# A decoder layer on one core: each head pair's weights scaled by their own sums of squares instead of by a scan of all weights

## The chip, the cores and the metric

The kernel runs on 1 core of a Trainium2 chip. The metric is device time in microseconds (us): the median of three runs of the kernel before is 2708.12 us (2706.8 to 2715.74).

## The reference

For 4 batches of 1024 tokens by 1024 features, x gets three updates, each after a layer norm without parameters:

```python
x = x + attn(norm(x))    # 16 heads of 64, causal; qkv = x @ w_qkv; softmax; out @ w_out
x = x + xattn(norm(x))   # softmax((ctx Wq + bq)(ctx Wk + bk)^T), 1024 x 1024, applied along the features
x = x + ffn(norm(x))     # 8 experts: gate by squared projections, best expert's rank-8 update, blended by the gate
```

Everything is float32. The kernel computes each large product with float16 pairs: an operand is a rounded high part plus the rounded rest, and a product is three matmuls (high by high, high by low, low by high). Float16 has a small range, so a weight tile is first multiplied by a power of two found from the weights themselves.

## The kernel before

The program is a list of steps per engine. Five strings per phase (`PE_START`, `DVE_START` and so on for the start; `..._BODY` for each head pair; `..._TAIL` for a batch's last pair with all that follows it) give the order on TensorE, VectorE (DVE), ScalarE (ACT), GpSimd (POOL) and the DMA queue of SyncE (SP). `walk` goes through them; a `+` after a name means the next pair, `++` the one after it; `ONCE` hangs further steps behind a step of one pair. Nothing reorders them: an engine that waits at a step holds back all its later ones. Attention goes by 8 head pairs per batch (n = 0 to 31; weights are prepared only for n below 8 and read back from DRAM copies later).

The start of batch 0 brings eight x tiles (128 tokens by 1024) into transposed pairs. For tile i: `AI` loads it, `AB` takes the statistics (DVE, bn), `AS` makes the scale and the shift (three tiny POOL instructions ve, rs, sh), `AX` normalizes (ACT), `AH` rounds (POOL, to probs), `AL` takes the rest (DVE, to probs), `AT` is a DMA transpose into `xt`. `x_in` has two slots, tile i + 2 is loaded after `AL` of tile i.

The weights of pair n are three tiles t = 0, 1, 2 (q, k, v; 128 x 1024): `WI` loads one to `w_raw` (two slots), `WH` rounds it with the scale `up_w` (POOL), `WL` takes the rest (DVE), `WS` stores the pair to DRAM. The scale is one for all q tiles, one for all k and one for all v, so the start first reads all 24 tiles of w_qkv: `SI` loads one into the large buffers r2 and r3 that attention needs later, `SR` takes its largest absolute value (DVE, tile_max, L985), and `SC1` to `SC3` reduce eight such columns (a PE transpose, a maximum, a power of two: `scale`, L887 to L911). w_out's eight tiles are scanned in pairs 0 and 1 (four SI loads behind `T1`, four SR behind `R6`), and prepared in pairs 3 to 6 (VI, VH, VL, VS).

`P t h` is a projection: 24 matmuls of 512 columns for weight tile t and half h of the tokens, in four parts; `CH` (ACT) and `CL` (DVE) move its result to float16 pairs. Then for the row blocks q = 0 to 7 of a pair: `S q` scores (PE), `X q` row maxima (DVE; the first of a pair is L850 of shape 128x128), `E q` exp with its sum (ACT, two instructions), `R q` reciprocals, `H q` rounding (POOL, pn), `L q` rest (DVE, pn), `T q` DMA transpose of pn (two slots), and `M0`, `M1` the products with v, with `OH` and `OL` behind them. `V` is the DMA transpose of v. `constants` (`CS`) builds the expert constants: 16 float32 matmuls and the scale of the expert weights.

Of the kernel before, what the change touches and what calls it, by code (L numbers as in the profile page):

```python
# [122 lines left out]
for pair in range(3, 7):
    u, v = 2 * pair - 6, 2 * pair - 5
    ONCE["SP", pair, "T1"] = f"VI{u} VI{v}"
    ONCE["POOL", pair, "H31"] = f"VH{u} VH{v}"
    ONCE["DVE", pair, "R4"] = f"VL{u} VL{v}"
    ONCE["SP", pair, "T5"] = f"VS{u} VS{v}"
# [11 lines left out]
def decoder_layer(nc, x, w_qkv, w_out, ctx_t, w_ctx, b_ctx, w_ffn, v_ffn, w_up, center, slope, out):  # L140
    es = ExitStack()
    with es:
# [19 lines left out]
        neg_half = sb(es, "neg_half", [P, 1])  # L162
        bias_c = sb(es, "bias_c", [P, 2])
        tile_max = sb(es, "tile_max", [P, 40])
        part_max = sb(es, "part_max", [P, 8])
        whole_max = sb(es, "whole_max", [P, 8])
        least_max = sb(es, "least_max", [P, 8])
        power = sb(es, "power", [P, 8])
        inverse = sb(es, "inverse", [P, 8])
        up_w = sb(es, "up_w", [P, 8])  # L170
        back = sb(es, "back", [P, 4])
        sc, c_out, c_ffn, c_ffn2 = (back[:, i:i + 1] for i in range(4))
# [163 lines left out]
        def proj_bank(n, h):  # L336
            return ps_s[:, 0, half(h)] if n % PAIRS == 0 else ps_p[:, h, :]

        def scale_bank(j):
            return ps_p[:, 0, 0:P] if j < 4 else ps_o[:, 1, 0:P]  # L340
# [42 lines left out]
        with nc.Block() as block:  # L383

            @block.sync
            def _(sp):
# [53 lines left out]
                def rest(kind, a, b):  # L440
                    if kind == "SI":
                        j, i = a
                        if j < 3:
# [9 lines left out]
                        return
# [761 lines left out]
```

## Time and profile before

| what | value |
|---|---|
| median of 3 runs | 2708.12 us |
| profiled execution | 2711.69 us, span 2709.8 us |
| PE busy | 2395.8 us (88%) |
| DVE busy | 1890.0 us (70%) |
| ACT busy | 780.1 us (29%) |
| POOL busy | 713.2 us (26%) |
| DMA | 403.97 MB, mean 149 GB/s |

Busy times are shares of the whole span. PE at 88% on average says little about the first 5% of the span: the profile's slices show PE at 0, 5, 8, 8 tenths there and 9 in most later ones. The stages must be read apart, and the times in them refer to the span's start.

### The profile page before, as it was taken

How to read it: one execution, taken by the hardware profiler on the slowest of the kernel's cores; microseconds unless marked ns; L12 is line 12 of the kernel's file. 1: busy time of each engine (PE TensorE's matmuls, PEld its weight loads, DVE VectorE, ACT ScalarE, POOL GpSimd, SP SyncE). 2: the span in 40 equal slices, each digit the busy share in tenths (PEclk: the TensorE clock that was granted, in tenths of full speed). 3: DMA queues.
4: the chain of work that ended last, by engine and by line, in shares of the span. 5: the costliest groups of instructions: out<-in, count | busy, mean ns of one | idle time of the engine just before them, and what ended most of it. 6: DMA issues, size and time to landing. Idle time of an engine off the chain costs nothing.

```text
span 2709.8 us, 37859 instructions
## 1 busy us (share of the span) xinstructions
PE 2395.8 (88%) x14389; PEld 1180.2 (44%) x14389; DVE 1890.0 (70%) x3421; ACT 780.1 (29%) x1557; POOL 713.2 (26%) x981
## 2 busy tenths in 40 slices
PE   0588888799898999979988999979989999988997
PEld 0233434354454444445444444445444444435544
DVE  4577877756876777765785777675696777765566
ACT  1033333321213333332212333342121333342110
POOL 3132433213402222212421222222430222222220
PEclk6799999899999999989998999989999999998997
DMA  6677778866746676786753777685773677777543
GB/s 174 227 179 170 170 199 200 210 148 146 145 105 126 138 145 142 146 201 139 154 118 100 143 143 145 143 197 128 160 146 107 119 145 146 142 149 185 109 78 93
DMA packets 986009, 403.97 MB, mean 149 GB/s; under 512 B 937116, under 2 KB 946332, under 8 KB 985828
## 3 DMA queue, kind: packets, MB, share of 16 engines
q1 hardware_dynamic: 985828, 401.56, 67.4%
q8 instruction: 114, 1.87, 0.3%
q14 instruction: 67, 0.55, 0.1%
HBM read 133.05 MB, written 33.55 MB: 61 GB/s over the span
## 4 chain that ended last, share of the span: by engine, by line
PE 60%; DVE 19%; DMA 9%; issue 5%; ACT 3%; POOL 2%; SPq 1%; ACTq 0%; POOLq 0%; DVEq 0%
PE ps_p L538 8%; PE ps_p L540 8%; PE ps_p L539 8%; DMA r<-pn 7%; PE ps_s L538 7%; PE ps_s L539 7%; PE ps_s L540 7%; PE ps_s L583 6%; PE ps_o L608 5%; DVE pn L817 4%; DVE peak L854 2%; ACT probs L743 2%; DVE bn L822 2%; DMA qk<-in_x 2%; PE ps_s L588 1%
## 5 line engine op out<-in xcount | busy, mean ns | idle before, releaser
L1081 POOL TENSOR_SCALAR pn<-probs,rden 128x640 f16<-128x640 f32 (+7 forms) x512 | 388.9, 772 | 1294.5 <-DVE rden L866 774.2
L743 ACT ACTIVATE probs<-ps_s,low,back 128x640 f32<-128x640 f32 (+7 forms) x512 | 421.4, 826 | 887.3 <-DVE low L857 775.8
L817 DVE SCALAR_TENSOR_TENSOR pn<-probs,rden,pn 128x640 f16<-128x640 f32 (+7 forms) x512 | 474.6, 959 | 170.1 <-POOL pn L1081 170.1
L538 PE MATMUL ps_p<-r,w 128*128 128x512 f16 x1344 | 514.5, 383 | 2.6 <-DVE qk L817 2.6
L539 PE MATMUL ps_p<-r,w 128*128 128x512 f16 x1344 | 513.9, 382 | 0.0
L540 PE MATMUL ps_p<-r,w 128*128 128x512 f16 x1344 | 513.5, 382 | 0.0
L583 PE MATMUL ps_s<-qk 64*128 64x512 f16 (+3 forms) x2304 | 245.5, 339 | 118.6 <-ACT probs L743 108.6
L854 DVE TENSOR_REDUCE peak<-ps_s 128x2 f32<-128x1280 f32 (+3 forms) x128 | 241.4, 1886 | 40.5 <-PE ps_s L588 37.6
L608 PE MATMUL ps_o<-r,vn 128*64 128x512 f16 (+3 forms) x2304 | 213.2, 342 | 44.2 <-issue 43.7
L583 PEld LDWEIGHTS ps_s<-qk 64*128 64x128 f16 x2304 | 91.8, 97 | 266.3 <-ACT probs L743 156.7
L540 PEld LDWEIGHTS ps_p<-r,w 128*128 128x128 f16 x1344 | 132.3, 98 | 161.7 <-issue 5.3
L608 PEld LDWEIGHTS ps_o<-r,vn 128*64 128x64 f16 x2304 | 141.3, 114 | 132.8 <-issue 80.6
L538 PE MATMUL ps_s<-r,pn 128*128 128x512 f16 x512 | 195.0, 381 | 0.0
L540 PE MATMUL ps_s<-r,pn 128*128 128x512 f16 x512 | 194.7, 380 | 0.0
L539 PE MATMUL ps_s<-r,pn 128*128 128x512 f16 x512 | 194.7, 380 | 0.0
L538 PEld LDWEIGHTS ps_p<-r,w 128*128 128x128 f16 x1344 | 132.5, 99 | 142.2 <-DVE qk L817 4.5
L539 PEld LDWEIGHTS ps_p<-r,w 128*128 128x128 f16 x1344 | 132.4, 98 | 137.4 <-issue 4.0
L538 PE MATMUL ps_s<-r 128*128 128x512 f16 x384 | 146.0, 380 | 0.0
L539 PE MATMUL ps_s<-r 128*128 128x512 f16 x384 | 145.6, 379 | 0.0
L540 PE MATMUL ps_s<-r 128*128 128x512 f16 x384 | 145.6, 379 | 0.0
L863 DVE TENSOR_SCALAR den_s<-den 128x2 f32<-128x2 f32 x256 | 42.5, 166 | 134.1 <-ACT probs L743 134.1
L1085 POOL TENSOR_SCALAR ve<-mv 128x1 f32<-128x1 f32 x96 | 28.5, 296 | 399.0 <-DVE mv L825 397.5
(167 smaller groups left out, 3532.0 us busy)
## 6 DMA issues: line engine op xcount, KB each, us to landing
w<-w_pairs SPq DMA_DIRECT2D x72, 512.0 KB, 3.9
qk<-in_x SPq DMA_DIRECT2D x32, 512.0 KB, 4.3
r<-wo_pairs SPq DMA_DIRECT2D x16, 1024.0 KB, 6.6
w_raw<-in_x SPq DMA_DIRECT2D x32, 512.0 KB, 4.1
out<-r SPq DMA_DIRECT2D x32, 512.0 KB, 2.9
r<-in_w_qkv SPq DMA_DIRECT2D x24, 512.0 KB, 5.7
w_raw<-in_w_qkv SPq DMA_DIRECT2D x24, 512.0 KB, 5.8
w_pairs<-w SPq DMA_DIRECT2D x24, 512.0 KB, 5.5
```

The costliest lines, as they stand in the source:

```text
L538: pe.matmul(ps, lh, rh, start=start and k == ks[0], stop=False)
L539: pe.matmul(ps, lh, rl, start=False, stop=False)
L540: mm = pe.matmul(ps, ll, rh, start=False, stop=stop and k == ks[-1])
L583: pe.matmul(ps_s[:, j, to.start + c:to.start + d], qk_part(n, 0, qs, block_of(q))[rows(j), :], qk_part(n, 1, ks, slice(c, d))[rows(j), :], ...
L608: mm = pe.matmul(ps_o[rows(j), g, c:HALF], vn[:, n % 2, vs, kb, rows(j)], keys_of(g, j, s, kb), start=kb == 0 and vs == 0 and s == 0, stop ...
L743: act.activation(probs_part(q, j, w), ps_s[:, j, scores(q)], ACT.Exp, bias=low[:, n % 2, i:i + 1], scale=sc, accum_out=den[:, n % 2, i:i + ...
L817: dve.scalar_tensor_tensor(out=to, in0=bank, scalar=scale, in1=rounded, op0=ALU.mult, op1=ALU.subtract).then_inc(ok, 1)
L822: ins = dve.bn_stats(bn[:, T % 2, h, :], src[:, half(h)])
L854: dve.tensor_reduce(peak[:, n % 2, r], ps_s[:, :, scores(q)], AX_X, ALU.max).then_inc(peak_ok, 1)
L863: dve.tensor_scalar(den_s[:, n % 2, r], den[:, n % 2, r], 1.0 / UP_A, None, ALU.mult).then_inc(den_ok, 1)
L1081: pool.tensor_scalar(to, src, scale, 1.0, ALU.mult, ALU.mult).then_inc(ok, 1)
L1085: pool.tensor_scalar(ve, mv[:, 1:2], EPS, UP_X ** -2, ALU.add, ALU.mult).then_inc(ok_ve, 1)
```

## The change

The scan of w_qkv goes. ACT takes the sum of squares of each raw tile of a pair (`WN`, activation Square with `accum_out`, written beside into scratch called junk), three PE transposes (`WC` on PE) and a chain of small DVE instructions (`WC` on DVE, `own_scales`) make the pair's own three powers of two from it. Pair n + 2 is treated in the body of pair n, pairs 0 and 1 in the start. The softmax scale is one column per pair (`sc(n)`). The eight x tiles of batch 0 have eight slots (`x1`, in r2, free now), so their loads wait for nothing. Pair 0 projects P00, P10, P20 first (first half of the tokens) and then P01, P11, P21; its two banks alternate by `turn_of`. The expert constants move behind the last x tile. w_out is still scanned for one common scale, together with the v tiles of pairs 4 to 7, by ACT (`SI`, `SN`, twelve tiles in pairs 0 and 1). `WI`, `WS` and `VI` stand at other places between the transposes `T`. From batch 1 on nothing changes.

DVE, start, around x tile 3: before (bn, mv: statistics of an x tile; tile_max: the scan; probs: `AL`).

```order
L985 TENSOR_REDUCE tile_max<-r 128x1
L1002 TENSOR_TENSOR probs<-qk_1,probs 128x1024
L822 BN_STATS bn<-qk_1 128x6 x2
L825 BN_AGGR mv<-bn 128x2
L985 TENSOR_REDUCE tile_max<-r 128x1
L1002 TENSOR_TENSOR probs<-qk_1,probs 128x1024
```

Now, with the scale chain of pair 0 (c_peak, c_low and c_den_s are its temporaries, sizes holds the scales):

```order
L883 BN_STATS bn<-r 128x6 x2
L886 BN_AGGR mv<-bn 128x2
L1089 TENSOR_TENSOR probs<-r,probs 128x1024
L950 TENSOR_REDUCE c_peak<-ps_o 128x3
L953 TENSOR_SCALAR c_low<-c_peak 128x3
L955 TENSOR_SCALAR sizes<-c_low 128x3
L960 RECIPROCAL c_den_s<-sizes 128x3
L966 TENSOR_SCALAR sizes<-c_den_s 128x3
L967 TENSOR_SCALAR sizes<-sizes 128x1
L883 BN_STATS bn<-r 128x6 x2
L886 BN_AGGR mv<-bn 128x2
L1089 TENSOR_TENSOR probs<-r,probs 128x1024
```

The scan's row is gone from each tile's turn, and one chain of six small rows stands between tiles.

ACT, end of pair 0: before (probs: `E`; qk, vt: `CH`).

```order
L743 ACTIVATE probs,den<-ps_s,low,back 128x896 x2
L732 ACTIVATE qk_1<-ps_p 128x512
L743 ACTIVATE probs,den<-ps_s,low,back 128x1024 x2
L732 ACTIVATE vt<-ps_p 128x512
L743 ACTIVATE probs,den<-ps_s,low,back 128x128 x2
L732 ACTIVATE vt<-ps_p 128x512
```

Now, with the sums of squares of scanned tiles (L813, from xn and t):

```order
L796 ACTIVATE probs,den<-ps_s,low,sizes 128x896 x2
L813 ACTIVATE r,sizes<-xn 128x8x128
L776 ACTIVATE qk_1<-ps_p 128x512
L796 ACTIVATE probs,den<-ps_s,low,sizes 128x1024 x2
L813 ACTIVATE r,sizes<-t 128x8x128 x2
L776 ACTIVATE vt<-ps_p 128x512
L796 ACTIVATE probs,den<-ps_s,low,sizes 128x128 x2
L776 ACTIVATE vt<-ps_p 128x512
```

Two sums stand between the last exp of the pair and the copy of v's first half.

The DMA queue (SP), first half of pair 1: before (r<-pn: `T`; 128x4x128 is T0, 128x8x128 T1).

```order
L424 DMA_TRANSPOSE r<-pn 128x4x128
L424 DMA_TRANSPOSE r<-pn 128x8x128
L452 DMA xn<-in_w_out 128x1024 x2
L452 DMA t<-in_w_out 128x1024 x2
L401 DMA w_pairs<-w 128x2048
L395 DMA w_raw<-in_w_qkv 128x1024
L424 DMA_TRANSPOSE r<-pn 128x12x128
L424 DMA_TRANSPOSE r<-pn 128x16x128
```

Now:

```order
L454 DMA_TRANSPOSE r<-pn 128x4x128
L475 DMA xn<-in_w_out 128x1024
L475 DMA t<-in_w_out 128x1024
L475 DMA t<-in_w_qkv 128x1024
L431 DMA w_pairs<-w 128x2048
L454 DMA_TRANSPOSE r<-pn 128x8x128
L426 DMA w_raw<-in_w_qkv 128x1024
L454 DMA_TRANSPOSE r<-pn 128x12x128
L431 DMA w_pairs<-w 128x2048
L426 DMA xn<-in_w_qkv 128x1024
L454 DMA_TRANSPOSE r<-pn 128x16x128
```

Four transfers stand ahead of T1 instead of none, five ahead of T2 instead of six, and seven ahead of T3 instead of six. In pair 2 it is one, two and four instead of none, two and two.

The diff, cut:

```diff
 ACT_BODY = """
-    E00 E01 CH21 E10 E11 E20 E21 CH00+ E30 E31 OH1- E40 E41 CH01+ E50 E51 CH10+ OH0 E60 E61 CH11+ E70 E71
+    E00 E01 CH21 E10 E11 WN0++ E20 E21 CH00+ WN1++ E30 E31 OH1- E40 E41 CH01+ WN2++ E50 E51 CH10+ OH0 E60 E61
...
 PE_START = """
-    CS SC0 SC1 P000+ P001+ P002+ P003+ P010+ P011+ P012+ P013+ SC2 P100+ P101+ P102+ P103+ P110+ P111+ P112+ P113+
-    SC3 P200+ P201+ P202+ P203+ P210+ P211+ P212+ P213+ S0+ S1+
+    WC+ P000+ P001+ P002+ P003+ P100+ P101+ P102+ P103+ P200+ P201+ P202+ P203+ CS SC0 P010+ P011+ P012+ P013+
+    P110+ P111+ P112+ P113+ WC++ P210+ P211+ P212+ P213+ S0+ S1+
 DVE_START = """
+    AB0+ AB1+ AL0+ AB2+ AL1+ AB3+ AL2+ AB4+ AL3+ WC+ AB5+ AL4+ WL0+ AB6+ AL5+ WL1+ AB7+ AL6+ WL2+ CL00+ AL7+ CL10+
+    CS CL20+ SC0 CF CL01+ CL11+ WC++ CL21+ WL0++ WL1++
 ACT_START = """
+    AX0+ AX1+ AX2+ WN0+ AX3+ WN1+ AX4+ WN2+ AX5+ AX6+ AX7+ CH00+ CH10+ CH20+ CH01+ WN0++ WN1++ CH11+ WN2++ CH21+
 POOL_START = """
+    AS0+ AS1+ AH0+ AS2+ AH1+ AS3+ AH2+ AS4+ AH3+ WH0+ AS5+ AH4+ WH1+ AS6+ AH5+ WH2+ AS7+ AH6+ AH7+ CF WH0++ WH1++
 SP_START = """
+    AI0+ AI1+ WI0+ AI2+ WI1+ AI3+ WI2+ AI4+ AI5+ AT0+ AI6+ AT1+ AI7+ AT2+ CS AT3+ AT4+ AT5+ AT6+ AT7+ WI0++ WI1++
+    WI2++ WS0+ WS1+ WS2+ WS0++ V+
...
+for pair, first in ((0, 0), (1, 6)):
+    for at, row in (("T0", (0, 1, 2)), ("T4", (3,)), ("T5", (4,)), ("T6", (5,))):
+        ONCE["SP", pair, at] = " ".join(f"SI{first + e:02d}" for e in row)
+    for at, row in (("E31", (0,)), ("E41", (1,)), ("E51", (2,)), ("E61", (3,)), ("E71", (4, 5))):
+        ONCE["ACT", pair, at] = " ".join(f"SN{first + e:02d}" for e in row)
...
+        def turn_of(n, t, h):
+            return 6 * n + (3 * h + t if n == 0 else 2 * t + h)
+        def raw(n, t):
+            if n == 0 or n == 1 and t == 2:
+                return first_raw[:, 3 if n else t, :]
+            return w_raw[:, t, :] if t < 2 else xn3[:, 1, :]
+        def x_in(T):
+            return x1[:, T, :] if T < TB else c_probs[:, T % 2, :]
...
                     if kind == "WI":
-                        if k >= 2:
-                            sp.wait_ge(w_ok, k - 1)
+                        if n >= 3 or n == 2 and t < 2:
+                            sp.wait_ge(w_ok, 3 * n + t - 2)
...
+                    elif kind == "WC":
+                        pe.wait_ge(own_ok, 3 * n + 3)
+                        for t in range(3):
+                            mm = pe.transpose(ps_o[:, 1, block_of(t)], sum_of(n, t).broadcast_to([P, P]), ident[:, :])
+                        mm.then_inc(own_turn, 1)
...
+                    elif kind == "WN":
+                        act.wait_ge(w_in[t], 16 * (n + 1))
+                        act.activation(junk(n), raw(n, t).rearrange("p (t d) -> p t d", t=TB), ACT.Square, scale=NORM,
+                                       accum_out=sum_of(n, t)).then_inc(own_ok, 1)
...
+                if kind == "SN":
+                        act.wait_ge(scan_in[e % 3], 16 * (e // 3 + 1))
...
+                def own_scales(n):
+                    c = 3 * n
+                    dve.wait_ge(own_turn, n + 1)
+                    powers(slice(c, c + 3), (ps_o[:, 1, 0:3 * P], True), own_step, 4 * n)
+                    dve.tensor_scalar(up_w[:, c:c + 3], inverse[:, :], 2.0 ** 13, None, ALU.mult)
+                    dve.tensor_scalar(sc(n), power[:, c:c + 1], power[:, c + 1:c + 2], 2.0 ** -15, ALU.mult,
+                                      ALU.mult)
```

## Rows read from the trace of the kernel before

**Rows 1.** Windows: PE, PEld, DVE, ACT, POOL busy, clock, DMA share, GB/s.

```profile
0.00:136.60 136.60, 42.72 (x180) 19.83 (x180) 69.28 (x102) 14.79 (x15) 34.44 (x59) 0.71 0.65 199
136.60:512.50 375.90, 327.69 (x2072) 150.23 (x2072) 292.74 (x460) 125.62 (x278) 131.46 (x138) 0.97 0.78 182
189.00:248.10 59.10, 47.72 (x305) 22.61 (x306) 44.15 (x69) 18.10 (x40) 17.54 (x20) 0.97 0.75 178
248.10:299.40 51.30, 47.42 (x305) 21.42 (x305) 41.55 (x72) 18.31 (x40) 18.55 (x20) 0.97 0.76 157
817.20:1150.70 333.50, 317.69 (x2068) 146.61 (x2070) 237.42 (x417) 126.37 (x278) 82.28 (x112) 0.99 0.71 139
```

**Rows 2.** Chain of waits, one x tile: start, us, engine and tile.

```profile
26.25 3.96 DMA qk<-in_x
30.23 1.30 DVE bn L822 x2
...
31.76 1.08 DVE tile_max L985
32.84 1.14 DVE probs L1002
```

**Rows 3.** Timeline of x tiles: start, us, engine, line, work [idle before, releaser].

```profile
4.48 1.29 DVE L822 BATCH_NORM_STATS2 bn<-qk 128x6 f32<-128x512 f32 x2 [4.48 <-DMA qk<-in_x]
...
22.30 0.27 POOL L1089 TENSOR_SCALAR sh<-mv,rs 128x1 f32<-128x1 f32 x1
...
23.92 1.04 POOL L1081 TENSOR_SCALAR probs<-qk 128x1024 f16<-128x1024 f32 x1
...
32.77 1.34 POOL L1089 TENSOR_SCALAR sh<-mv,rs 128x1 f32<-128x1 f32 x1
...
34.14 1.24 ACT L759 ACTIVATE qk<-qk,sh,rs 128x1024 f32<-128x1024 f32 x1 [9.03 <-POOL sh L1089]
```

**Rows 4.** Timeline from the scan's first scale to the first row maxima.

```profile
76.59 0.47 PE L630 MATMUL ps_p<-ident,part_max 128*128 128x128 f32 x1 [58.65 <-DVE part_max L884]
...
78.33 1.12 POOL L1081 TENSOR_SCALAR w<-w_raw,up_w 128x1024 f16<-128x1024 f32 x1 [3.12 <-DVE up_w L901]
...
79.55 1.28 DVE L817 SCALAR_TENSOR_TENSOR w<-w_raw,up_w,w 128x1024 f16<-128x1024 f32 x1 [1.39 <-POOL w L1081]
...
80.89 0.61 PE L538 MATMUL ps_s<-r,w 128*128 128x512 f16 x1 [3.83 <-DVE w L817]
...
87.86 0.60 ACT L732 ACTIVATE qk<-ps_s 128x512 f16<-128x512 f32 x1 [13.78 <-PE ps_s L540]
...
93.04 0.60 ACT L732 ACTIVATE qk<-ps_s 128x512 f16<-128x512 f32 x1 [4.58 <-PE ps_s L540]
...
136.60 0.28 DVE L850 TENSOR_REDUCE peak<-ps_s 128x1 f32<-128x128 f32 x1
```

**Rows 5.** Timeline of the expert constants on PE.

```profile
12.08 3.95 PE L617 MATMUL ps_p<-ffn_prod,ones 128*128 128x136 f32 x16 [12.08 <-DVE ffn_prod L919]
```

**Rows 6.** Chain of waits in pair 0: the scan of w_out.

```profile
175.66 4.49 DVE tile_max L985 x4
```

**Rows 7.** Timelines of DVE and SP at the end of pair 0.

```profile
182.79 2.28 DVE L854 TENSOR_REDUCE peak<-ps_s 128x2 f32<-128x2048 f32 x1
...
182.89 4.25 SPq L424 DMA_TRANSPOSE r<-pn  x1
```

**Rows 8.** Timelines of POOL in pair 1, and of SP and ACT in pair 2.

```profile
222.04 1.57 POOL L1081 TENSOR_SCALAR pn<-probs,rden 128x640 f16<-128x640 f32 x2 [10.68 <-DMA r<-pn]
...
271.15 19.62 SPq L424 DMA_TRANSPOSE r<-pn  x4
...
275.71 0.99 ACT L743 ACTIVATE probs<-ps_s,low,back 128x768 f32<-128x768 f32 x1 [3.03 <-DVE low L857]
```

**Rows 9.** DMA issues: KB each, median us to landing.

```profile
w_raw<-in_w_qkv SPq DMA_DIRECT2D x24, 512.0 KB, 5.8
```

**Rows 10.** Timeline of ACT at the start.

```profile
0.71 1.28 ACT L759 ACT_TABLE_LOAD   x1 [0.71 <-PEq L1208]
```

More of the change, by code:

```diff
@@ L32 @@
 UP_X, UP_A = 2.0 ** 10, 2.0 ** 14
-Q_OUT = 2.0 ** -19
+NORM = 2.0 ** -24
+Q_OUT = 2.0 ** -17
 O_OUT = 2.0 ** -14
@@ L121 @@
+for pair in range(3, 7):
+    u, v = 2 * pair - 6, 2 * pair - 5
+    ONCE["SP", pair, "T0"] = f"VI{u}"
+    ONCE["DVE", pair, "R1"] = f"VF{u}"
+    ONCE["POOL", pair, "H31"] = f"VH{u}"
+    ONCE["DVE", pair, "R4"] = f"VL{u}"
+    ONCE["SP", pair, "T4"] = f"VI{v}"
+    ONCE["POOL", pair, "H61"] = f"VH{v}"
+    ONCE["SP", pair, "T5"] = f"VS{u}"
+    ONCE["DVE", pair, "R7"] = f"VL{v}"
+    ONCE["SP", pair, "T7"] = f"VS{v}"
 for pair in range(PAIRS - 2, BATCH * PAIRS, PAIRS):
     ONCE["SP", pair, "T6"] = "JI0 JI1 KI"
[L123 to L128, printed above, removed]
@@ L161, in decoder_layer @@
         rank = sb(es, "rank", [P, EXPERTS])
[L162 to L172, printed above, removed]
+        sizes = sb(es, "sizes", [P, 104])
+        squares, power, up_w, back = sizes[:, 0:36], sizes[:, 36:63], sizes[:, 63:90], sizes[:, 90:101]
+        neg_half, bias_c = sizes[:, 101:102], sizes[:, 102:104]
+        c_out, c_ffn, c_ffn2 = (back[:, PAIRS + i:PAIRS + i + 1] for i in range(3))
         bn1, bn2, bn3 = (sb(es, f"bn{s}", [P, 2, 2, 6]) for s in (1, 2, 3))
@@ L274, in decoder_layer @@
         m_ok, oh_ok, o_ok = sems("m_ok oh_ok o_ok")
+        a_first = [sem(f"a_first{s}") for s in range(TB)]
         a_in = [sem(f"a_in{s}") for s in range(2)]
@@ L334, in scores, with proj_bank, junk, sum_of @@
             return slice(base, base + (q + 1) * P)
[L336 to L340, printed above, removed]
+        def turn_of(n, t, h):
+            return 6 * n + (3 * h + t if n == 0 else 2 * t + h)
+        def proj_bank(n, t, h):
+            return ps_s[:, 0, half(turn_of(n, t, h) % 2)] if n % PAIRS == 0 else ps_p[:, h, :]
+        def raw(n, t):
[4 more added lines that the diff above has]
+            return x1[:, T, :] if T < TB else c_probs[:, T % 2, :]
+        def junk(n):
+            return pt[:, 8 * SEQ:9 * SEQ].rearrange("p (t d) -> p t d", t=TB) if n < 2 else o16[:, :, 0, PAIRS - 1, :]
+        def sum_of(n, t):
+            c = 8 * t + n if n < 4 or t < 2 else 32 + n - 4
+            return squares[:, c:c + 1]
+        def scan_sum(e):
+            c = 24 + e if e < 8 else 12 + e
+            return squares[:, c:c + 1]
+        def scale(n, t):
+            return up_w[:, 3 * n + t:3 * n + t + 1]
+        def sc(n):
+            return back[:, n % PAIRS:n % PAIRS + 1]
         def ctx_bank(t):
@@ L750, in attend @@
                         if n == 0:
-                            act.wait_ge(scan_ok, 24)
+                            act.wait_ge(a_lo, TB)
                         act.activation(heads_out(g, 0, p), heads_bank(g), ACT.Copy, scale=O_OUT).then_inc(oh_ok, 1)
                 def rest(kind, a, b):
+                    if kind == "SN":
+                        e = 10 * a[0] + a[1]
+                        act.wait_ge(scan_in[e % 3], 16 * (e // 3 + 1))
+                        if e > 0:
+                            act.wait_ge(scan_ok, e)
+                        act.activation(o16[:, :, 1, PAIRS - 1, :], wo_scan[e % 3].rearrange("p (t d) -> p t d", t=TB), ACT.Square,
+                                       scale=NORM, accum_out=scan_sum(e)).then_inc(scan_ok, 1)
+                        return
                     i, = a if a else (0,)
```

293 lines of the change are left out of this document (155 added, 138 removed), and 3 rows, old and new, of the table ONCE.

## The prediction

> **What bounds the kernel now.** I first cut the span into stages by windows [rows 1]. PE is busy for 42.7 of the first 136.6 us, for 327.7 of the 375.9 us of pairs 0 to 6, and for 317.7 of the 333.5 us of the same seven pairs in batch 1. So the start is 94 us of PE idle, batch 0's pairs carry 42 us more than those of batch 1, and from there on PE is nearly full and the change touches nothing. The limit at 136.6 is the first row maxima of pair 0 (X0) [rows 4]; all that the start must deliver is in front of it.
>
> Then the chain of waits for one x tile [rows 2]: load 3.96, statistics 1.30 (with their sum to 31.76), scan 1.08, rest 1.14, and the next load starts. That is a ring of 7.7 us because a slot is loaded only after its rest: the scan and the load are both in it. The projections [rows 4]: the first scale's transpose is at 76.59, POOL's rounding at 78.33, the matmuls start at 80.89, the first result is moved at 87.86, the next at 93.04. A group of 24 matmuls thus takes 5.2 us when PE comes from work and 7.0 after an idle time. The groups of k and v wait for the scans of 16 more tiles; last of all X0 at 136.60.
>
> **The start after the change.** With eight slots the load leaves the ring; the scan leaves it too. What is left per tile is in the written orders: on DVE `AB(i+1) AL(i)`, on POOL `AS(i+1) AH(i)`. So AH(i) stands behind AS(i+1), that behind AB(i+1), and that behind AL(i-1): a ring of statistics 1.5, three POOL instructions 1.3 (1.0 from the end of the statistics at 31.76 to sh at 32.77, and 0.27 for a free sh), rounding 1.04, rest 1.22 [rows 2, 3], with gaps 5.2 us. The normalization (1.24) runs a tile ahead and is hidden.
>
> First tile: lands at 4.48 [rows 3], and 1.5 + 1.3 + 1.25 + 1.1 + 1.2 gives its rest at 11. Three rings: tile 3 done at 26.5.
> Scales of pair 0: the third sum of squares, a 1024-column activation like the normalization (1.25, and about 0.1 for its accumulator), ends at about 27. The old chain needs 1.74 from transpose to POOL [rows 4]; three transposes and three rows wide I take 3: POOL starts at 30.
> Tiles 4 to 6 with one WH and one WL each: DVE does AB, AL, WL (1.5 + 1.2 + 1.28), POOL AS, AH, WH (1.2 + 1.04 + 1.12), in a ring of 6.3 that now has WL in it: WL2 ends at 30 + 3 x 6.3 = 49.
> PE: P00 and P10 are done by then. P20 also needs the rest of P00 (0.7 behind WL2): 49.6 to 54.8. The constants stand behind it: their DVE work is done by 53, so PE has them from 54.8 to 58.8 (3.95 us [rows 5]), and 0.8 for a copy and a transpose. P01 and P11: 10.4 us to 70.0. Tile 7's transpose, issued at about 51, has landed long before. Then PE stands at `WC++` for the third sum of squares of pair 1, which ACT takes only behind the copy of P11: 0.6 + 1.35 and semaphores, plus three transposes of 0.3, 3.3 us in all. P21 5.2 to 7.0, its move 1.4, and two WL (2.4) ahead of X0: 73.3 + 6.1 + 1.4 + 2.4 = 83.
>
> So X0 goes from 136.6 to 83: **53.6 us less**. Bounds: if WL and AL hide and PE goes straight on, 76; if each of the eight tiles goes on costing 7.7 us, the last rest is at 73 instead of 51 and X0 at 105. I take 83, since every term has a row.
>
> A port rule bears on this. In the trace POOL's sh takes 1.34 us instead of 0.27 when it meets DVE's rest [rows 3]. The Trainium skill (SBUF — State Buffer, Who interferes with whom) says that a DVE instruction with two SBUF inputs and a GpSimd instruction that reads SBUF exclude each other, the first to issue keeping the port, while tensor_reduce never contends; by that rule the removed scan never slowed POOL, and each WL and AL that remains can hold a WH or AH for up to its 1.2 us. The trace agrees with the first half: beside the scan (31.76 to 32.84 [rows 2]) ve and rs are done by 32.77 [rows 3]. My ring has DVE and POOL mostly one behind the other, so the sum holds by the row; by the rule at its worst, six such holds put X0 at 90.
>
> **The pairs of batch 0.** Removed: four DVE scans in pair 0 and four in pair 1, 4.49 us on the chain [rows 6]: -4.5 each, -9 together. Moved on SP: in pair 1 T2 stood behind six transfers, and POOL waited 10.68 us for it [rows 8]; with five ahead, but three of them issued before T1, T1 is late instead. I take -3 for pair 1, and -4 for pair 0, where T1 comes late anyway and only one load is left ahead of T2.
>
> Added, in the order of the body. (1) `WN2++` on ACT in front of E50: its tile is loaded behind T2. In pair 2 T2 is issued from 271.15 [rows 8], so the load goes at about 275 and lands at 279 to 281 (5.8 us is its median [rows 9]); with 1.35 for the sum, E50 starts at about 281 instead of 275.71 [rows 8]. Queued behind it on ACT are E50, E51 and the copies, and PE's S6 waits for E51. But PE has P and M0 there until about 280 and DVE is at L40 and L41, so of the 5 us I count 1.5. (2) The chain `WC++` on DVE between X6 and L50, 1.5 us, of six pairs (n = 0 to 5). X6 now stands ahead of L50, so E6 runs beside it: L50 and T5 are later by 3 or more, X7 by about 1.5. I count 1 to 2. Together +3 in pair 2 and, where VI was already in the way and is now split, +1 each in pairs 3 to 5. (3) At the end of pairs 0 and 1 ACT has SN04 and SN05 in front of `CH20+`. SI05 is issued behind T6; T6 took 4.25 us to issue, from 182.89, when X7 began at 182.79 [rows 7]. So the load goes at 4.4 us after X7's start, lands at 8 and its sum ends at 9.5; copy and rest, then X0 of the next pair at 10.5 instead of 6.2 (189.0 less 182.8 [rows 1, 7]). I count 3.5 of the 4.3, since POOL gets ahead meanwhile: +7 for the two.
> (4) ACT as an engine has room: 125.6 busy of 375.9 us [rows 1], and 30 more sums add 40.
>
> Sum per pair: 0: -4.5 - 4 + 3.5 + 2 = -3; 1: -4.5 - 3 + 3.5 + 1 = -3; 2: +3; 3 to 5: +3; 6: 0. **Zero in all.** Bounds: -17 if all seven pairs fall to the 51.3 us of pair 2, which had no scan loads; +20 if the sums of squares cost their full 5 us in pairs 1 to 5 (the ends of the unshown waits).
>
> Profiled execution 2711.7 less 53.6 is 2658; it lies 3.6 above the median, and the same difference from the median 2708.1 gives 2654.5. I say **2655**.
>
> **Rivals.**
> *The start stays slow.* Loads, stores and transposes share the queue; SP needs about 3.5 us per transpose, and if POOL waits for the probs slots each tile costs 7.7 again: X0 at 105, time 2677. For it: the DMA share was 0.65 over the start [rows 1]. Against: that share was mostly the scan's 12 MB, which is gone. 10%.
> *The pairs gain too.* If the scattered transfers shorten the wait for T2 (10.68 in pair 1, while pair 2 without scan loads takes 51.3 against 59.1 [rows 1]), batch 0's seven pairs lose 12 to 18 us: 2637 to 2643. For it: the difference of pairs 1 and 2. Against: the same megabytes, and four v tiles more. 15%.
> *Slower.* ACT in front of E50 behind a load: the place is `WN2++` in six pairs and SN in two. It decides from 54 / 6 = 9 us lost per pair; with the longest wait for a transfer in the trace, 10.7 us, in each, 64 us come back and the time is 2719. Against: PE and DVE cover part of each wait. 3%.
> *Table switches.* If Square and Exp did not share ACT's function table, each of some 28 groups of sums among the exps would bring two loads, of 1.28 us as the one at the start took [rows 10]: 72 us in front of exps that PE waits for, and a time of 2709 to 2727. The Trainium skill (ScalarE: Activation LUTs, Table sets: the hidden batching unit) tells to batch activations by table set for that reason, and with its about 2.7 us a switch it would be more. The changed program has one table load on ACT, as before, so 1%, at about 2720.
> *It doesn't do what it says:* the first tile's chain takes as long because constants and x share the queue: X0 no earlier than 125, 2697. 2%.
>
> **How the numbers follow.** The forecast holds 69%: 2645 to 2668. Two kernels within 0.3% (8 us) can't be told apart. Slower by more: the 3% and the 1%. Within: 1%, from a slow start and slow pairs together. Faster: 95%. The range for 8 in 10 takes in the pair bounds and half of the slow start: 2634 to 2676.
>
> **What would show it.** Right: X0 of pair 0 (the 128x128 row maxima on ps_s) at 83 +- 5; x tiles' rests spaced 5.2 us, later 6.3; PE idle for 2 to 3 us before the last projection of pair 0; ACT idle before sums of squares waiting for a DMA; pairs 0 to 6 in 370 to 380 us; everything after pair 7's start as long as before (2197 us from there to the end of the span). Wrong: X0 above 95, or the pairs' sum off by more than 15.

## The result, and the profile after: slower, with the start as forecast and the pairs far off

| what | before | after |
|---|---|---|
| median | 2709.14 us (2706.8 to 2715.74, 4 runs) | 2749.32 us (2739.13 to 2750.7, 4 runs) |
| ratio | | 1.0136, 95% interval 1.0106 to 1.0167 |
| profiled execution | 2711.69 us, span 2709.8 | 2750.7 us, span 2748.8 |

The forecast was 2655 with a range of 2634 to 2676: the change was expected to save 54 us and cost 40. The windows of the kernel after, cut at the first row maxima (X0) of pairs 0, 1, 2, 3 and 7 (columns as in [rows 1]), show where:

```profile
0.00:79.80 79.80, 39.02 (x183) 18.10 (x183) 43.08 (x70) 21.01 (x27) 26.59 (x59) 0.99 0.66 178
79.80:143.80 64.00, 48.60 (x259) 20.59 (x259) 36.01 (x67) 26.46 (x56) 17.78 (x19) 0.82 0.71 171
143.80:220.40 76.60, 52.41 (x307) 23.09 (x307) 39.26 (x70) 27.43 (x58) 17.09 (x19) 0.81 0.68 152
220.40:286.20 65.80, 48.93 (x302) 22.03 (x303) 40.71 (x78) 21.10 (x46) 14.32 (x17) 0.86 0.57 124
...
549.80:2748.80 2199.00, 2032.55 (x12132) 1010.24 (x12130) 1513.25 (x2863) 640.07 (x1264) 547.16 (x786) 0.96 0.65 140
```

```profile
79.80:549.80 470.00, 347.85 (x2098) 155.78 (x2099) 286.76 (x493) 156.39 (x338) 133.01 (x137) 0.86 0.67 150
```

The start went from 136.6 to 79.8 us, 56.8 less. Pairs 0 to 6 went from 375.9 [rows 1] to 470.0, 94.1 more. Everything from pair 7's first row maxima on takes 2199.0 instead of 2709.8 - 512.5 = 2197.3. Sum: -56.8 + 94.1 + 1.7 = +39.0, the difference of the two spans. Pair 2 alone takes 65.8 us instead of 51.3 [rows 1], with 302 matmuls in its window against 305.

**The start.** Its rows answer to [rows 2 to 4]. Timeline of the kernel after (start, us, engine, line, work, idle time before and its releaser): statistics of two x tiles, the first scale's maxima, the first rounding, the first projection, two rests and a rounding behind the second; then the constants and the end of the start.

```profile
10.72 1.28 DVE L883 BATCH_NORM_STATS2 bn<-r 128x6 f32<-128x512 f32 x2
...
15.69 1.28 DVE L883 BATCH_NORM_STATS2 bn<-r 128x6 f32<-128x512 f32 x2
...
26.76 0.56 DVE L950 TENSOR_REDUCE c_peak<-ps_o 128x3 f32<-128x384 f32 x1 [1.05 <-PE ps_o L606]
...
28.38 1.12 POOL L1168 TENSOR_SCALAR w<-r,sizes 128x1024 f16<-128x1024 f32 x1 [3.92 <-DVEq L969]
...
32.23 1.12 POOL L1168 TENSOR_SCALAR w<-r,sizes 128x1024 f16<-128x1024 f32 x1
32.28 2.14 DVE L1089 TENSOR_TENSOR probs<-r,probs 128x1024 f16<-128x1024 f32 x1 [2.31 <-POOL probs L1168]
...
35.67 0.61 PE L563 MATMUL ps_s<-r,w 128*128 128x512 f16 x1 [8.95 <-DVE w L878]
...
46.44 1.23 DVE L1089 TENSOR_TENSOR probs<-r,probs 128x1024 f16<-128x1024 f32 x1 [2.31 <-POOL probs L1168]
...
46.76 1.80 POOL L1168 TENSOR_SCALAR probs<-r 128x1024 f16<-128x1024 f32 x1 [0.36 <-ACT r L820]
...
55.49 2.02 PE L659 MATMUL ps_p<-ffn_prod,ones 128*128 128x136 f32 x16
...
70.36 0.54 PE L606 MATMUL ps_o<-ident,sizes 128*128 128x128 f32 x3 [1.72 <-ACT r L784]
...
77.42 2.47 DVE L878 SCALAR_TENSOR_TENSOR w<-w_raw,sizes,w 128x1024 f16<-128x1024 f32 x2
...
79.81 0.29 DVE L914 TENSOR_REDUCE peak<-ps_s 128x1 f32<-128x128 f32 x1
```

The ring of an x tile is 15.69 - 10.72 = 4.97 us (worked out: 5.2), POOL's first rounding starts at 28.38 (30), P20 runs from 50.3 (49.6), two WL stand in front of X0, and X0 is at 79.81 (83). With a WL in it the ring is longer than forecast: the rests of x tiles 4 and 5 start at 32.28 and 39.36, 7.1 us apart (6.3), which eats up the earlier start of the weights. The 3.2 us by which X0 is early come mainly from two terms. The constants took 2.02 us instead of the 3.95 of [rows 5], and PE stood at `WC++` for less: P21 starts 2.1 us after the end of P11 (3.3 were counted), 1.72 of them idle.

**The pairs.** The groups of waits between 79.8 and 549.8 (engine, tile, line, what it waited for: us in total, times, longest):

```profile
PE ps_s L623 <- ACT probs L796: 117.8, 29, 15.8
...
ACT r L784 <- DMA w_raw<-in_w_qkv: 96.8, 12, 11.2
...
ACT r L784 <- DMA xn<-in_w_qkv: 30.7, 6, 5.7
```

The same view of the kernel before, from 136.6 to 512.5:

```profile
PE ps_s L583 <- ACT probs L743: 34.8, 26, 3.3
```

L784 is the sum of squares. ACT stands 18 times in front of it, 127.5 us in all, and PE's wait for the exps grew from 34.8 to 117.8. The timelines of SP, ACT, PE and DVE in pair 2 show the three places, and what PE and DVE make of them:

```profile
223.58 4.88 SPq L454 DMA_TRANSPOSE r<-pn  x1
228.56 2.03 SPq L459 DMA_TRANSPOSE vn<-vt  x1
230.65 0.91 SPq L426 DMA_DIRECT2D w_raw<-in_w_qkv  x1
236.63 1.19 SPq L454 DMA_TRANSPOSE r<-pn  x1
...
240.15 1.23 SPq L454 DMA_TRANSPOSE r<-pn  x1
241.43 0.57 SPq L426 DMA_DIRECT2D w_raw<-in_w_qkv  x1
252.90 1.43 SPq L454 DMA_TRANSPOSE r<-pn  x1
...
255.28 0.42 SPq L426 DMA_DIRECT2D xn<-in_w_qkv  x1
```

```profile
234.83 1.06 ACT L784 ACTIVATE r<-w_raw 128x1024 f16<-128x1024 f32 x1 [8.25 <-DMA w_raw<-in_w_qkv]
235.79 0.19 ACT L784 ACTIVATION_READ_ACCUMULATOR r<-w_raw 128x1 f32 x1
235.89 0.65 ACT L796 ACTIVATE probs<-ps_s,low,sizes 128x384 f32<-128x384 f32 x1
...
245.20 1.06 ACT L784 ACTIVATE r<-w_raw 128x1024 f16<-128x1024 f32 x1 [7.43 <-DMA w_raw<-in_w_qkv]
...
261.21 1.06 ACT L784 ACTIVATE r<-xn 128x1024 f16<-128x1024 f32 x1 [5.13 <-DMA xn<-in_w_qkv]
```

```profile
232.13 4.41 PE L650 MATMUL ps_o<-r,vn 128*64 128x512 f16 x48
...
247.92 1.78 PE L623 MATMUL ps_s<-qk 64*128 64x512 f16 x12 [11.38 <-ACT probs L796]
```

```profile
239.64 0.48 DVE L878 SCALAR_TENSOR_TENSOR pn<-probs,rden,pn 128x256 f16<-128x256 f32 x1
```

Read them together. SP issues T7, V, then WI0 at 230.65; the tile lands at 234.8, and `WN0++`, which stands in front of E20, has held ACT for 8.25 us by then. WI1 is issued at 241.43, behind T1; `WN1++`, in front of E30, ends its wait at 245.20, and PE, which had nothing left after `M1-` (L650, to 236.54), has by then idled most of its 11.38 us for exps. WI2 stands behind T2 and holds E50 for 5.13 us. Behind each sum stand exps whose scores are ready, behind these PE's next scores, DVE's reciprocals and rests, and behind those the next transpose and so the next load. T1 is an example: it is issued at 240.15, right behind DVE's rest of row block 1 (L11, 239.64 + 0.48 = 240.12). That rest stands in DVE's list behind R2, which needs the exps that `WN0++` had held.

### The profile page after: what moved, and what is told of

It reads as the page before. It is cut to its first block, busy times and chain, and to the rows that moved or that the text cites. A ratio compares the mean times of both kernels' runs of the same rounds, so it can differ in the third digit from the quotient of the medians.

```text
span 2748.8 us, 38004 instructions
## 1 busy us (share of the span) xinstructions
PE 2419.4 (88%) x14411; PEld 1184.1 (43%) x14411; DVE 1843.1 (67%) x3423; ACT 817.5 (30%) x1629; POOL 706.8 (26%) x981
## 4 chain that ended last, share of the span: by engine, by line
PE 56%; DVE 19%; DMA 9%; issue 7%; ACT 4%; POOL 3%; SPq 2%; ACTq 0%; POOLq 0%; DVEq 0%
PE ps_p L563 8%; PE ps_p L564 8%; PE ps_p L565 8%; DMA r<-pn 7%; PE ps_s L563 7%; PE ps_s L564 6%; PE ps_s L565 6%; PE ps_s L623 6%; DVE pn L878 5%; PE ps_o L650 4%; ACT probs L796 3%; DVE peak L918 2%; DMA w_raw<-in_w_qkv 2%; DVE bn L883 2%; PE ps_s L628 1%
## 5 line engine op out<-in xcount | busy, mean ns | idle before, releaser
L796 ACT ACTIVATE probs<-ps_s,low,sizes 128x640 f32<-128x640 f32 (+7 forms) x512 | 420.9, 825 | 824.4 <-DVE low L921 714.6
L878 DVE SCALAR_TENSOR_TENSOR pn<-probs,rden,pn 128x640 f16<-128x640 f32 (+7 forms) x512 | 455.1, 926 | 140.2 <-POOL pn L1168 138.8
L563 PE MATMUL ps_p<-r,w 128*128 128x512 f16 x1344 | 520.6, 387 | 2.4 <-DVE qk L878 2.4
L564 PE MATMUL ps_p<-r,w 128*128 128x512 f16 x1344 | 520.3, 387 | 0.0
L565 PE MATMUL ps_p<-r,w 128*128 128x512 f16 x1344 | 519.0, 386 | 0.0
L650 PE MATMUL ps_o<-r,vn 128*64 128x512 f16 (+3 forms) x2304 | 212.5, 341 | 30.9 <-issue 30.8
L650 PEld LDWEIGHTS ps_o<-r,vn 128*64 128x64 f16 x2304 | 133.5, 114 | 125.8 <-issue 67.1
```

The lines of the kernel that those rows point to most:

```text
L563: pe.matmul(ps, lh, rh, start=start and k == ks[0], stop=False)
L564: pe.matmul(ps, lh, rl, start=False, stop=False)
L565: mm = pe.matmul(ps, ll, rh, start=False, stop=stop and k == ks[-1])
L650: mm = pe.matmul(ps_o[rows(j), g, c:HALF], vn[:, n % 2, vs, kb, rows(j)], keys_of(g, j, s, kb), start=kb == 0 and vs == 0 and s == 0, stop ...
L796: act.activation(probs_part(q, j, w), ps_s[:, j, scores(q)], ACT.Exp, bias=low[:, n % 2, i:i + 1], scale=sc(n), accum_out=den[:, n % 2, i: ...
L878: dve.scalar_tensor_tensor(out=to, in0=bank, scalar=scale, in1=rounded, op0=ALU.mult, op1=ALU.subtract).then_inc(ok, 1)
```

## Experiments

Each experiment edits the changed kernel unless it says otherwise. Those run once are judged by the length of pairs 0 to 6 in the profile, since a single total can't settle a few us. The start is 79.6 to 79.9 us in all of them. Everything from pair 7 on is the same work in all of them; it took 2186.7 to 2199.0 us, 0.6% apart. If the pairs scatter by the same share, that is 2 to 3 us (an estimate), so differences of that size between two windows say little.

**All loads of the sums early (e1).** On SP only (the start's list gets one more `WI0+++` at its end):

```diff
-    WD2+ WI0++ T0 WS1+ T1 WI1++ T2 WS2+ WI2++ T3 T4 WD0++ T5 T6 WS0++ WD1++ T7 V+
+    WD2+ WI1++ WI2++ T0 WS1+ T1 T2 WS2+ T3 T4 WD0++ T5 T6 WS0++ WI0+++ WD1++ T7 V+
```

> Only the SP order differs from the changed kernel: of pair n + 2 the loads WI1 and WI2 stand ahead of T0 and WI0 stands ahead of T7 of the body before, instead of WI0 ahead of T0, WI1 behind T1 and WI2 behind T2. The same sums, chains and transfers remain. Theory A (ACT stands at WN0, WN1 and WN2 for loads that SP issues only behind gated transposes; 96.8 + 30.7 us of such waits in pairs 0 to 6): nearly all waits go, pairs 0 to 6 fall from 470 us to 375 to 400, the time to 2655 to 2680. Rival B (the sums as work on ACT, 30 x 1.25 us, and the scale chain cost it): waits go, but the pairs stay above 450, time 2730 to 2750. Rival C (stores and loads ahead of T1 to T3 delay the transposes): only a part, 430 to 450, time about 2715.

2680.38 us (2671.18 to 2682.98, 4 runs) against 2710.61 of the kernel before: ratio 0.9894 (0.9877 to 0.9912). Window of pairs 0 to 6, and the waits in it:

```profile
79.80:480.40 400.60, 338.53 (x2098) 151.78 (x2099) 288.99 (x493) 156.05 (x338) 137.38 (x137) 0.94 0.76 176
```

```profile
ACT r L784 <- DMA w_raw<-in_w_qkv: 27.5, 6, 6.5
```

Same instructions, same bytes, another place in one queue: 470.0 becomes 400.6, so 69.4 of the 94.1 us come with the late loads (the medians are 68.9 apart). Theory A had 375 to 400 and at most 2680, and the run lies at that edge; B and C are far off. The wait for a tile in `xn` (WI2) is gone from the list. For tiles in `w_raw` ACT still waits 27.5 us, so not every wait went.

**No sums from pair 2 on (e2), and no scale chain either (e3).** The loads stay where the changed kernel has them. The main lines of the edits; the waits and columns that go with them are left out:

```diff
 e2, ACT, step WN:
-                        if n >= PAIRS:
+                        if n >= 2:
 e3 besides, DVE, step WC (PE's the same; the scales are those of pair n % 2):
-                        if n < PAIRS:
+                        if n < 2:
```

> The changed kernel without the sums of squares of pairs 2 to 7 (their scales come from the sums of pairs 0 and 1, the common one of v and w_out from half the tiles); loads, stores, chains and w_out's sums stay where they are. Theory A and rival B both expect pairs 2 to 5 to lose their excess (about 68 us each now, then 52 to 56), total near 2670; only against e1 does it tell the waits from the work: A expects e1 and this one within 15 us, B expects this one 40 us or more below e1. Rival C expects pairs 2 to 5 to stay at 62 or more.

> As the one without the sums of pairs 2 to 7, and without their scale chains on PE and DVE too (all take the scales of pairs 0 and 1). The difference to it is the price of six chains, 1.5 us of DVE each: theory A expects 0 to 9 us less (1 to 2 per pair), a rival that sees PE and DVE held at the chain expects 20 us or more.

Windows of pairs 0 to 6, e2 and then e3:

```profile
79.60:479.50 399.90, 341.20 (x2098) 153.39 (x2099) 290.63 (x492) 138.91 (x302) 136.62 (x137) 0.93 0.77 176
```

```profile
79.80:467.30 387.50, 333.73 (x2080) 149.83 (x2081) 279.15 (x457) 138.53 (x302) 137.47 (x137) 0.95 0.79 182
```

Taking the sums away (399.9) and loading for them early (400.6) come to the same, as theory A said; rival B wanted 40 us between them. So neither ACT's 17 us of work for the sums, nor the 27.5 us that ACT still waits in e1, nor a late load that only POOL's WH needs (e2) shows a cost. That two of these cancel is not excluded. The loads are as late in e2 as in the changed kernel, and the pairs are fast all the same: late transfers by themselves, rival C, are not the cause; the sums in front of the exps are. The six chains in pairs 0 to 5 cost 12.4 us, 2.1 each; 0 to 9 had been expected, and 20 or more by the rival. (Totals of the single runs: 2674.29 and 2661.04.)

**Only WI2 late (e6); only WI0 early (e9); only WI1 early (e10).**

```diff
 e6, from e1:
-    WD2+ WI1++ WI2++ T0 WS1+ T1 T2 WS2+ T3 ...
+    WD2+ WI1++ T0 WS1+ T1 T2 WS2+ WI2++ T3 ...
 e9:
-    WD2+ WI0++ T0 WS1+ ... T6 WS0++ WD1++ T7 V+
+    WD2+ T0 WS1+ ... T6 WS0++ WI0+++ WD1++ T7 V+
 e10:
-    WD2+ WI0++ T0 WS1+ T1 WI1++ T2 ...
+    WD2+ WI0++ WI1++ T0 WS1+ T1 T2 ...
```

> As e1, but the load WI2 of pair n + 2 stays behind T2 as in the changed kernel; WI0 and WI1 are early. It isolates the one ACT wait that the prediction priced (WN2 ahead of E50: 5 us late, 1.5 counted). By that price pairs 0 to 5 are 9 us above e1 (400.5), at 410; if the full wait falls on the path, 30 above, at 430; the rest of the 70 us between the changed kernel and e1 belongs to WN0 and WN1, which the prediction left out.

> Changed kernel with one load moved on SP: WI0 of the pair after next is issued ahead of T7 and V, a pair earlier, instead of behind them; WI1 and WI2 stay behind T1 and T2. Known so far: pairs 0 to 6 take 470.0 us in the changed kernel, 407.8 with WI0 and WI1 early, 400.5 with all three. Theory A (each wait of ACT costs by itself, and the two of 8.3 and 7.4 us in pair 2 share the 62 us between 470 and 408 about as their lengths): this run loses 28 to 38 us, pairs 432 to 442. Theory B (the waits hide one another: whichever load is late, PE falls behind as far): it loses under 12, pairs above 458. Theory C (WI0 alone does it, since the wait for it is the longest and falls where PE has least in hand): 50 or more less, pairs under 420.

> Changed kernel with one load moved on SP: WI1 is issued ahead of T0 and T1 instead of behind them; WI0 stays behind T7 and V, WI2 behind T2. Theory A (each wait costs by itself): this run loses the rest of the 62 us, 24 to 34, pairs 436 to 446, and the two gains of this pair of runs add up to about 62. Theory B (the waits hide one another): under 12 less, pairs above 458, the two gains together far under 62. Theory C (WI0 alone): pairs above 458, while the other run is under 420.

Windows of pairs 0 to 6 of e6, e9 and e10 (single totals 2682.05, 2734.24, 2703.89):

```profile
79.90:487.70 407.80, 344.76 (x2098) 153.84 (x2099) 289.98 (x492) 156.09 (x338) 137.62 (x137) 0.92 0.75 173
```

```profile
79.90:545.70 465.80, 351.32 (x2098) 157.02 (x2099) 285.15 (x493) 156.66 (x338) 132.28 (x137) 0.87 0.67 152
```

```profile
79.90:507.30 427.40, 347.43 (x2098) 156.80 (x2099) 290.39 (x492) 156.64 (x338) 133.91 (x137) 0.91 0.73 165
```

| loads behind transposes | pairs 0 to 6 |
|---|---|
| all three (changed kernel) | 470.0 |
| WI1, WI2 (e9) | 465.8 |
| WI0, WI2 (e10) | 427.4 |
| WI2 (e6) | 407.8 |
| none (e1) | 400.6 |

WI2's wait is worth 7.2 us in six pairs (9 had been expected for e6). Removing WI0's alone saves 4.2, removing WI1's alone 42.6, both 62.2: neither additive (28 to 38 and 24 to 34 were the guesses) nor "all in WI0"; only the part "WI0 alone saves under 12" of theory B held. The ACT timelines of pair 2 say why, e9 and then e10:

```profile
246.96 1.06 ACT L784 ACTIVATE r<-w_raw 128x1024 f16<-128x1024 f32 x1 [12.84 <-DMA w_raw<-in_w_qkv]
```

```profile
219.55 1.06 ACT L784 ACTIVATE r<-w_raw 128x1024 f16<-128x1024 f32 x1 [8.31 <-DMA w_raw<-in_w_qkv]
...
222.38 1.06 ACT L784 ACTIVATE r<-w_raw 128x1024 f16<-128x1024 f32 x1
```

The waits are gates in series. Pair 2 of e9 begins at 221.8, so its `WN1++` starts 25.2 us into the pair; in the changed kernel it is 245.20 - 220.4 = 24.8. T1, and WI1 behind it, comes hardly sooner: 19.3 us into the pair (e9, at 241.11) instead of 19.7. In the changed kernel T1 waits for DVE's rest, as shown above. In e9 that rest is done at 235.9, but T1 also stands behind T0, and T0 is issued just when PE's `M1-` ends: at 239.21 in e9, where `M1-` ends at 239.12, and at 236.63 in the changed kernel, where it ends at 232.13 + 4.41 = 236.54. ACT merely waits 12.84 us in one place instead of 8.25 and 7.43 in two. With WI1 early, only the gate 14.5 us into the pair is left (219.55 - 205.1), and it costs (427.4 - 407.8) = 19.6 us in the pairs instead of 62.

**w_out and the v tiles not scanned (e4).** The lines that hang the steps in go (the waits for them too):

```diff
-        ONCE["SP", pair, at] = " ".join(f"SI{first + e:02d}" for e in row)
+        pass
-        ONCE["ACT", pair, at] = " ".join(f"SN{first + e:02d}" for e in row)
+        pass
```

> The changed kernel without the scan of w_out and of the last v tiles (no SI, no SN; their common scale comes from four v tiles). Pairs 0 and 1 take 64.0 and 76.6 us now. My step (3) priced SN05 behind T6 at 3.5 us for each pair: if that and the sums' work are all, they fall by 8 to 10 together; if the three loads ahead of T1 and the waits for them carry the excess of pair 1 over pair 2, pair 1 falls to 66, and the total by 12 to 18, to about 2733.

Pairs 0 and 1 take 58.3 and 67.9 us instead of 64.0 and 76.6, 14.4 less; pairs 2 to 6 stay within 1.5 us each; sum 455.9 (total of the one run 2735.03). The scan is a small part, and only in its own two pairs. The fall is in the second guess, 12 to 18, not in the first, 8 to 10.

**The sixth scan sum of each pair put into the next pair (e7, from e1).**

```diff
-    for at, row in (("E31", (0,)), ("E41", (1,)), ("E51", (2,)), ("E61", (3,)), ("E71", (4, 5))):
+    for at, row in (("E31", (0,)), ("E41", (1,)), ("E51", (2,)), ("E61", (3,)), ("E71", (4,))):
+    ONCE["ACT", pair + 1, "E11"] = f"SN{first + 5:02d}"
```

> As e1, but the last sum of pairs 0 and 1 (SN05, SN11), whose load stands behind T6, goes from the pair's end to the next pair's E11. The prediction's step (3) priced its wait ahead of CH20 at 3.5 us a pair: pairs 0 to 2 then take 5 to 8 us less together than in e1 (172.4). If the copy of v is not what X0 waits for, nothing changes.

```profile
79.90:472.30 392.40, 334.76 (x2097) 152.10 (x2098) 291.56 (x492) 155.75 (x338) 139.85 (x137) 0.95 0.78 180
```

Total of the one run 2669.11. The sum falls from 400.6 to 392.4; pairs 0 to 2 together, which hold both places, from 172.4 to 163.5, 8.9 less (5 to 8 had been expected): SN05 and SN11 in front of `CH20+` cost about 4.5 us each.

**An order made from this (e5), and the chain one step later (e8).** e5 issues the three loads ahead of T0, puts each sum one block of exps later, T1 right behind T0, and spreads the scan over three pairs. e8 is e5 with the scale chain behind L51, and with L50 ahead of X6 again as in the kernel before: two moves at once.

```diff
 e5, SP and ACT (the scan's places and waits with them):
-    WD2+ WI0++ T0 WS1+ T1 WI1++ T2 WS2+ WI2++ T3 T4 ...
+    WD2+ WI0++ WI1++ WI2++ WS1+ T0 T1 WS2+ T2 T3 T4 ...
-    E00 E01 CH21 E10 E11 WN0++ E20 E21 CH00+ WN1++ E30 E31 OH1- E40 ...
+    E00 E01 CH21 E10 E11 E20 E21 CH00+ WN0++ E30 E31 OH1- WN1++ E40 ...
 e8, DVE, from e5:
-    X5 L40 L41 R5 CL10+ X6 OL0 WC++ L50 L51 R6 ...
+    X5 L40 L41 R5 CL10+ L50 X6 OL0 L51 WC++ R6 ...
```

> Same computation as the changed kernel, other places for steps: the three loads of pair n + 2 and the store WS1 stand between V and T0 (SP waits there for M1 anyway), T1 follows T0 at once, the sums WN0, WN1 and WN2 stand one step later each on ACT, VI goes behind T1, and w_out's sums are spread over pairs 0 to 2, none behind a load that is issued less than one step ahead. Theory A with transposes delayed by transfers as the second cause (e1 left pairs 0 to 6 at 400.5 us, with 141 us of POOL waiting for transposes): pairs 0 to 6 at 375 to 390, time 2655 to 2670. Rival: the remainder of e1 is the work that the sums and chains add (e3 without sums and chains is at 387.5, against 400.5): then 395 or more and 2675 or more.

> As e5_order (383.8 us for pairs 0 to 6, median 2660.65), with DVE's scale chain moved from ahead of L50 to behind L51, ahead of R6, where DVE waits for E61; L50 is again ahead of X6 as in the kernel before. Theory: the chain's 1.5 us sits on the path L50, T5, H70 and costs 2 us in each of six pairs (e2 less e3: 12.5 us); in the wait for E61 it costs less than 1, so the pairs take 376 to 380 and the time is 2653 to 2659. Rival: X6 ahead of L50 is what pays (E6 starts earlier), and moving it back costs as much: 383 to 390 and no change or slower.

| kernel | median (lowest to highest, runs) | ratio to before (95%) |
|---|---|---|
| e5 | 2660.65 (2657.49 to 2666.95, 5) | 0.9819 (0.9801 to 0.9838) |
| e8 | 2659.12 (2657.87 to 2665.65, 5) | 0.9812 (0.9792 to 0.9833) |

Windows of pairs 0 to 6, e5 and then e8:

```profile
79.90:463.70 383.80, 336.47 (x2098) 151.15 (x2099) 294.11 (x493) 156.96 (x338) 139.18 (x137) 0.95 0.80 184
```

```profile
79.90:465.90 386.00, 336.32 (x2098) 153.16 (x2099) 296.09 (x493) 156.60 (x338) 137.90 (x137) 0.94 0.81 184
```

e5 beats the kernel before by 1.8% and the changed one by more: the whole idea in another order, inside what theory A gave it (375 to 390, 2655 to 2670). PE's wait for the exps is down to 47.1 us (34.8 before), though ACT still waits 27.8 us for loads of sums:

```profile
PE ps_s L622 <- ACT probs L795: 47.1, 27, 4.3
...
ACT r L783 <- DMA w_raw<-in_w_qkv: 27.8, 5, 6.5
```

e8 is the same as e5 within the measurement. Its theory (376 to 380 in the pairs) did not come true; 386.0 is what the rival said, for whom X6 ahead of L50 pays as much as the chain costs. Since e8 makes both moves, it does not show whether both are worth nothing or cancel. What keeps e5 7.9 us above the 375.9 of before is not taken apart further; its order differs from the changed kernel's in several places at once, so which of them gave how much of its gain over e1 (16.8 us) stays open too.

## Why the prediction was wrong

**What held.** The start: 79.8 for 83, 56.8 us less for 53.6. Its path is the one that was written down; its terms are off by up to 2 us, partly in opposite directions (above). Of its bounds, the 73 for the last rest counts eight rings of 7.7 us behind the first tile's rest at 11, where seven follow it: 65. The rest of the span took 2199.0 for 2197. No table switch: one table load on ACT, as said.

On the port, the trace shows a rest of 2.14 us (32.28) where POOL's rounding had started 0.05 us before it, and 1.23 (46.44) where none was running. Behind that second rest it was POOL's rounding (46.76) that took 1.80 us instead of the 1.04 of [rows 3]. The Trainium skill (SBUF — State Buffer, Who interferes with whom) says that a VectorE instruction with two SBUF inputs and a GpSimd instruction that reads SBUF contend, and that whoever issues first keeps the shared ports; the trace agrees. Two rests of x tiles (32.28, 39.36) became 0.9 us longer by it, and X0 still came ahead of the forecast, far from the 90 of six holds on the path.

**What failed first is step (1) of "Added, in the order of the body".** It names one sum, `WN2++` in front of E50, and prices it at 1.5 us. Each body has three: `WN0++` in front of E20 and `WN1++` in front of E30 were left out of the sum altogether, though the changed strings show them and SP's string shows their loads behind T7 and V and behind T1. For WN2 the price was about right: 7.2 us in six pairs (e6 against e1), 1.2 each, against the 1.5 counted. The two omitted ones cost 62.2 (changed kernel against e6). The prediction's own list of signs has "ACT idle before sums of squares waiting for a DMA" among those of being right: the waits were foreseen, but not what stands behind two of them. The argument used for WN2 (PE and DVE have work in hand) was never put to the other two places; at the second one PE has none, as its 11.38 us of idle time show.

Term by term, for pairs 0 to 6, as the steps from the kernel before over e3, e2, e1 and e6 to the changed kernel size them:

| step of the prediction | said | measured |
|---|---|---|
| WN0 behind V, WN1 behind T1 | left out | 62.2 (changed kernel less e6) |
| (1) WN2 behind T2 | +9 with (2) | 7.2 (e6 less e1) |
| (2) the chain WC | 1 to 2 per pair | 12.4, 2.1 per pair (e2 less e3) |
| (4) ACT's extra work | 0 | 0.7 (e1 less e2) |
| (3) SN in front of `CH20+` | +7 | +8.9 (e1 less e7) |
| scans gone, T2 earlier, pairs 0 and 1 | -16 | -2.6, net (e3) |
| pairs 2 to 6, nothing named | 0 | +5.3 (e3) |
| sum | 0 | 94.1 |

**The second failure is the credit of 16 us** (4.5 + 4 and 4.5 + 3 in pairs 0 and 1). In e3, with no sum of squares and no chain from pair 2 on, pairs 0 and 1 take 117.8 us against 52.4 + 59.1 = 111.5 before, 6.3 more; with 8.9 off for SN, only 2.6 of credit are left, net of whatever else was added there. No run takes it apart, nor the 5.3 us by which pairs 2 to 6 of e3 are longer than before; both are not far above the scatter of single runs. Third, (1) and (2) together came to 19.6 instead of 9, most of it the chain.

**The range.** Its upper bound, +20, was "the sums of squares cost their full 5 us in pairs 1 to 5", one wait per pair. The waits for loads cost 69.4 / 6 = 11.6 us in each of six pairs. Counting three waits of 5 us would have given 15 a pair, 90 in all. That is near the 94.1 only by luck: in e1 ACT's waits fell by 100 us (127.5 to 27.5) and the pairs by 69.4, and single waits do not add up (e9, e10). The slower rival had the right kind (ACT in front of exps behind a load) and the wrong place; it decides from 9 us per pair, and at 3% it was priced as the wait for one tile.

**The clock's part.** PE is busy 347.9 us for 2098 matmuls, against 327.7 for 2072 [rows 1], at a granted clock of 0.86 instead of 0.97. The added transposes of the chain are 3.0 of these 20 us; so about 17 of the 94 us show up as slower matmuls and not as idle time. PE waits 4.38 us up to 222.25; from there to 225.65 matmuls of 512 columns start 0.43 us apart, and from 225.9 on 0.21 us. The windows of the two stretches, with the granted clock (0.50, then 1.00: the levels of 1.2 and 2.4 GHz), and a matmul of each:

```profile
222.25:225.65 3.40, 3.40 (x14) 1.23 (x14) 3.33 (x10) 0.70 (x2) 0.72 (x2) 0.50 0.27 52
225.90:236.50 10.60, 10.60 (x81) 5.04 (x79) 3.33 (x8) 2.35 (x8) 0.93 (x2) 1.00 0.86 176
```

```profile
223.51 0.63 PE L563 MATMUL ps_p<-r,w 128*128 128x512 f16 x1
...
225.89 0.38 PE L563 MATMUL ps_p<-r,w 128*128 128x512 f16 x1
```

The forecast counted waits as their own length. In e1, with most waits gone, the clock is up at 0.94 and PE's busy time down at 338.5.

## What to carry to other kernels

Where each engine runs a written list, a step added to an engine with room can cost nothing for its work and much for its wait. For every added instruction, not the last one only, find the load it needs, what that load stands behind in its queue, what stands behind the instruction, and whether the bottleneck has work in hand meanwhile: the same kind of wait cost 1.2 us a pair in front of E50 and 10.4 in front of E20 and E30 together. If an early consumer is added to a load, move the load ahead of the transfers that wait for results; here that was worth 69 us, and it turned a loss of 1.4% into a gain of 1.1%. Waits of this kind stand in series, so removing the first may give next to nothing (4 us here) while a later one sets the pace (43 us): try each alone and all together.

## What had not been expected of the hardware

A sum of squares of a 128x1024 float32 tile with its accumulator takes ACT 1.06 + 0.19 us, but the next instruction starts 1.06 us after it (234.83, then 235.89), so the 30 of pairs 0 to 6 added 156.4 - 125.6 = 30.8 us of ACT work. For the 18 of them in e1 that e2 left out, pairs 0 to 6 were 0.7 us longer. The 16 small-output float32 matmuls of the constants took 2.02 us behind a busy PE and 3.95 after 12 us without work [rows 5]; the forecast took the latter. That is about the ratio of the clock's two levels, but the clock is not shown as the cause: the profile's granted clock reads 1.00 in both stretches. It also reads 1.00 at the first projections of the kernel after, whose matmuls take 0.61 to 0.63 us (35.67), so the column is no guide in the first 40 us, and neither is the 0.99 for the start.
